# First and last batch of a two-layer graph kernel in another order: weights by block, first x split on other engines, last attention re-ordered

## The reference

```
# layer 0:  Wi, Wj = W[:, :D], W[:, D:]        a = adj as float, deg = a.sum(1)
x = ln(x + deg * (x @ Wi.T + b) + a @ (x @ Wj.T))
# layer 1: 8 heads of 64, mask where adj == 0, scores / 8
q, k, v = x @ Wq.T + bq, x @ Wk.T + bk, x @ Wv.T + bv
p = softmax(where(adj == 0, -inf, q k.T / 8))
x = ln(x + (p v) @ Wo.T + bo)
```

## Time and profile before

| | us |
|---|---|
| median of 3 runs (3036.11 to 3036.71) | 3036.34 |
| the profiled execution's own time | 3034.67 |
| its span, first to last instruction | 3032.9 |
| PE busy in the span | 2974.3 (98%) |
| DVE / ACT / POOL busy | 2316.6 / 1729.0 / 1636.7 |
| mean granted TensorE clock | 0.992 |

### The profile page before, as it was taken

The page is one execution under the profiler, slowest core; times in us unless marked ns, Lnnn a source line. Parts: engine busy times, 40 slices in busy tenths (PEclk is TensorE's granted clock), DMA queues, the critical chain, the costliest instruction groups (busy, mean ns, idle before and its releaser), DMA issues.

```text
span 3032.9 us, 61054 instructions
## 1 busy us (share of the span) xinstructions
PE 2974.3 (98%) x20096; PEld 2618.4 (86%) x20096; DVE 2316.6 (76%) x5909; ACT 1729.0 (57%) x4620; POOL 1636.7 (54%) x1545
## 2 busy tenths in 40 slices
PE   5999999999999999999999999999999999999996
PEld 4888888888888888888888888888888888888886
DVE  6777777777777777777777777777777777777775
ACT  3555565565565555555655655555555556556554
POOL 5455555455555565555554555555655555545542
PEclk8999999999999999999999999999999999999998
DMA  3010100101101101101001011001001010010100
GB/s 125 29 42 28 35 35 28 41 28 35 41 28 35 41 28 35 41 28 35 32 30 41 28 35 41 28 35 41 28 35 36 33 35 29 33 41 28 35 29 22
DMA packets 48428, 108.37 MB, mean 36 GB/s; under 512 B 3600, under 2 KB 4112, under 8 KB 48400
## 3 DMA queue, kind: packets, MB, share of 16 engines
q1 hardware_dynamic: 48400, 108.02, 10.3%
HBM read 74.46 MB, written 33.55 MB: 36 GB/s over the span
## 4 chain that ended last, share of the span: by engine, by line
PE 97%; DVE 1%; issue 0%; ACT 0%; DMA 0%; POOL 0%; SPq 0%; POOLq 0%; DVEq 0%
PE proj L417 52%; PE proj L459 21%; PE av L417 8%; PE attn L575 7%; PE attn L563 7%; PE proj L513 2%; DMA w_raw<-in_w0T 0%; DVE wji_lo L1077 0%; ACT probs L719 0%; DVE probs L896 0%; DVE t_raw L1066 0%; DVE mj_mi L971 0%; DVE pT_lo L918 0%; DVE mj_mi L977 0%; DVE wq_lo L1082 0%
## 5 line engine op out<-in xcount | busy, mean ns | idle before, releaser
L719 ACT ACTIVATE probs<-probs,exp_bias 128x256 f32<-128x256 f32 x1024 | 508.0, 498 | 41.7 <-DVE exp_bias L904 40.6
L735 ACT CAST pT_hi<-attn 128x512 fp32r<-128x512 f32 x512 | 275.0, 588 | 379.8 <-PE av L417 318.7
L317 POOL TENSOR_TENSOR probs<-probs,row_inv 128x512 f32<-128x512 f32 x256 | 264.4, 1043 | 395.7 <-DVE row_inv L914 395.7
L918 DVE TENSOR_TENSOR pT_lo<-attn,pT_hi 128x512 fp32r<-128x512 f32 x512 | 328.7, 683 | 87.2 <-ACT pT_hi L735 85.2
L459 PE MATMUL proj<-wji_hi,xs_hi 128*128 128x512 f32 x896 | 363.4, 406 | 20.5 <-DVE wji_lo L1077 17.3
L896 DVE CUSTOM_DVE_ANT_0 probs<-attn,mask_add 128x256 f32<-128x256 f32 x1024 | 376.4, 419 | 6.3 <-PE attn L563 3.8
L459 PE MATMUL proj<-wji_lo,xs_hi 128*128 128x512 f32 x896 | 355.8, 397 | 0.0
L459 PE MATMUL proj<-wji_hi,xs_lo 128*128 128x512 f32 x896 | 355.7, 397 | 0.0
L928 DVE SCALAR_TENSOR_TENSOR oT<-av,bv_cols,o_part 64x256 f32<-64x256 f32 x512 | 243.4, 475 | 120.7 <-POOL oT_lo L345 60.5
L743 ACT COPY o_part<-av 64x512 f32<-64x512 f32 x256 | 149.5, 584 | 319.8 <-PE av L417 318.3
L345 POOL TENSOR_TENSOR oT_lo<-oT,oT_hi 128x256 fp32r<-128x256 f32 x256 | 201.6, 787 | 209.1 <-ACT oT_hi L750 209.1
(11 more groups left out here) (110 smaller groups left out, 8629.5 us busy)
## 6 DMA issues: line engine op xcount, KB each, us to landing
xs_raw<-in_xT SPq DMA_DIRECT2D x64, 512.0 KB, 3.3
xb<-in_x SPq DMA_DIRECT2D x64, 512.0 KB, 3.3
out<-hb SPq DMA_DIRECT2D x64, 512.0 KB, 2.8
w_raw<-in_w0T SPq DMA_DIRECT2D x2, 1024.0 KB, 7.2
stage<-in_wqT SPq DMA_DIRECT2D x1, 1024.0 KB, 12.3
stage<-in_wkT SPq DMA_DIRECT2D x1, 1024.0 KB, 14.5
stage<-in_wvT SPq DMA_DIRECT2D x1, 1024.0 KB, 5.3
stage<-in_woT SPq DMA_DIRECT2D x1, 1024.0 KB, 5.4
```

The lines of the kernel that those rows point to most:

```text
L317: pool.tensor_tensor(probs[:, g % 2, 1, :, :], probs[:, g % 2, 1, :, :], row_inv[:, g % 2, R:2 * R].unsqueeze(2).to_broadcast([P, R, N]), ...
L719: last = nc.scalar.activation(e, e, ACT.Exp, bias=exp_bias[:, g % 2, s:s + 1], scale=SCALE, accum_out=row_sum[:, g % 2, s:s + 1])
L735: nc.scalar.copy(pT_hi[:, i, :, :], attn[2 * (g % 2) + i][:, :].rearrange("p (k q) -> p k q", k=R)).then_inc(pt_hi_done, 1)
L918: V.tensor_tensor(pT_lo[:, i, :, :], attn[2 * (g % 2) + i][:, :].rearrange("p (k q) -> p k q", k=R), pT_hi[:, i, :, :].bitcast(F32), ALU.s ...
```

## The change

Head: `w0T` is loaded in four blocks of two DMAs of 256 KB each, each block with a semaphore of its own, and ACT and DVE wait for the block that they use. ACT makes the high halves of the first x, DVE its sums and low halves; POOL has no part in it. DVE splits weight block 0 before the first weight sum, and makes `deg` and `deg_b0` after the fourth `first_sum` instead of before the first. ACT makes wq's high half before `first_copy(0, 1)`. Of wq's low half POOL does one half of the columns after both `mi_add`, and DVE the other after the norm. The low halves of wv and wo stand one place later in DVE's list.

Tail: pairs 1 and 3 of the last batch write their transposed probabilities to a second pair of buffers (`mj_hi`, `mj_lo`, free by then), so `pt_high` need not wait for the `attend` before it. The second pair of heads' maxima stand before the first inverse sums; both y products come before the first transposes; the scores of pairs 2 and 3 are issued apart; on POOL `normalise_odd(b, 2)` stands before `split_o(b, 1)`.

```diff
+    W_LOADS = ((0, 0), (0, 1), (1, 1), (1, 0))
...
+        pT_tail = [(pT_hi, pT_lo), tuple(t[:, :, :].rearrange("p r (a n) -> p r a n", a=2) for t in (mj_hi, mj_lo))]
...
             load_xT(0)
-            for kind in range(2):
-                sp.dma_start(w_raw[:, kind, :, :], w0T[(1 - kind) * D:(2 - kind) * D, :].rearrange(
-                    "(c p) o -> p c o", p=P)).then_inc(w_loaded["wji"], 16)
+            for i, (kh, oh) in enumerate(W_LOADS):
+                for kind in range(2):
+                    at = (1 - kind) * D + kh * HD
+                    sp.dma_start(w_raw[:, kind, 2 * kh:2 * kh + 2, oh * HD:(oh + 1) * HD],
+                                 w0T[at:at + HD, oh * HD:(oh + 1) * HD].rearrange("(c p) o -> p c o", p=P)).then_inc(
+                                     block_loaded[i], 16)
...
-            sum_x(0)
-            for part in range(2):
-                x_high(0, part)
-                x_low(0, part)
+            mj_low_row1(0)
             pool.wait_ge(deg_b0_ready, R)
             add_bias(0)
-            mj_low_row1(0)
+            pool.wait_ge(mi_added, R)
+            pool.wait_ge(w_hi_done, 1)
+            pool.tensor_tensor(w_lo[WEIGHTS[0]][:, 0:2, :], stage[0][:, 0:2, :],
+                               w_hi[WEIGHTS[0]][:, 0:2, :].bitcast(F32), ALU.subtract).then_inc(w_half_split, 1)
             root("h", 0)
...
                 if not (first and pair == 0):
-                    pe.wait_ge(pt_read, 2 * (G * b + 2 * pair))
-                for g in (2 * pair, 2 * pair + 1):
+                    pe.wait_ge(pt_read, 2 * (G * b + pairs[-1] - 1))
+                for g in pairs:
...
             def last_step(b):
                 scores(b, 0)
                 y(b - 1, 0, tail=True)
+                y(b - 1, 1, tail=True)
                 transpose_p(b, 0, 0)
                 transpose_p(b, 0, 1)
-                attend(b, 0)
                 transpose_p(b, 1, 0)
                 transpose_p(b, 1, 1)
-                y(b - 1, 1, tail=True)
-                scores(b, 1)
-                attend(b, 1)
+                scores(b, 1, only=2)
+                attend(b, 0)
+                scores(b, 1, only=3)
+                attend(b, 1, tail=True)
...
-                    act.wait_ge(av_done, G * b + g)
+                    act.wait_ge(av_done, G * b + g - (1 if tail else 0))
...
-                    act.wait_ge(w_loaded["wji"], 32)
+                    act.wait_ge(block_loaded[(0, 3, 2)[blk]], 32)
...
+            for part, blocks in enumerate((slice(1, 4), slice(4, 8))):
+                if part == 0:
+                    act.wait_ge(xT_loaded, 16)
+                else:
+                    act.wait_ge(xs_summed, 4)
+                nc.scalar.copy(xs_hi[:, blocks.start - 1:blocks.stop - 1, :, :],
+                               xs_raw[:, blocks, :, :]).then_inc(xs_hi_done, 1)
             for i in range(4):
                 high_block(i)
...
+            split_weight(0)
             first_copy(0, 1)
-            split_weight(0)
...
+            dve.wait_ge(xT_loaded, 16)
+            x_ = lambda i: xs_raw[:, i, :, :]
+            V.tensor_tensor(x_(4), x_(0), x_(3), ALU.add).then_inc(xs_summed, 1)
+            V.tensor_tensor(x_(6), x_(1), x_(0), ALU.subtract).then_inc(xs_summed, 1)
...
+            x_low(0)
+            x_low(1)
+            low_block(0)
             sum_blocks(0)
-            low_block(0)
             sum_blocks(1)
...
             norm_apply("h", 0, h_row)
-            split_weight(1)
+
+            dve.wait_ge(w_hi_done, 1)
+            dve.wait_ge(w_half_split, 1)
+            V.tensor_tensor(w_lo[WEIGHTS[0]][:, 2:4, :], stage[0][:, 2:4, :], w_hi[WEIGHTS[0]][:, 2:4, :].bitcast(F32),
+                            ALU.subtract).then_inc(w_split, 1)
             hT_low(0, 0)
             hT_low(0, 1)
-            split_weight(2)
+            split_weight(1)
```

More of the change, by code:

```diff
@@ L549, in v, with scores @@
                 rows_times_w("v", r, hT_hi, hT_lo, "wv")
-            def scores(b, pair, first=False):
+            def scores(b, pair, first=False, only=None):
                 pe.wait_ge(read["q"], 2 * b + pair + 1)
                 pe.wait_ge(read["k"], 2 * b + pair + 1)
+                pairs = (2 * pair, 2 * pair + 1) if only is None else (only,)
                 if not (first and pair == 0):
-                    pe.wait_ge(pt_read, 2 * (G * b + 2 * pair))
-                for g in (2 * pair, 2 * pair + 1):
+                    pe.wait_ge(pt_read, 2 * (G * b + pairs[-1] - 1))
+                for g in pairs:
                     terms = [(q_hi, k_hi), (q_lo, k_hi), (q_hi, k_lo)]
@@ L577, in transpose_p, with attend @@
                 last.then_inc(pt_done, 1)
-            def attend(b, g, first=False):
+            def attend(b, g, first=False, tail=False):
                 if g == 0:
@@ L586, in attend @@
                 for i in range(2):
-                    terms = [(kt, half) for kt in range(R) for half in (pT_hi, pT_lo)]
+                    terms = [(kt, half) for kt in range(R) for half in pT_tail[g % 2 if tail else 0]]
                     for j, (kt, half) in enumerate(terms):
@@ L729, in normalise_even, with pt_high @@
                 last.then_inc(norm_even_done, 1)
-            def pt_high(b, g, i, first=False):
+            def pt_high(b, g, i, first=False, tail=False):
                 act.wait_ge(pt_done, 2 * (G * b + g) + i + 1)
                 if i == 0 and not (first and g == 0):
-                    act.wait_ge(av_done, G * b + g)
-                nc.scalar.copy(pT_hi[:, i, :, :],
+                    act.wait_ge(av_done, G * b + g - (1 if tail else 0))
+                nc.scalar.copy(pT_tail[g % 2 if tail else 0][0][:, i, :, :],
                                attn[2 * (g % 2) + i][:, :].rearrange("p (k q) -> p k q",
@@ L830, in last_step @@
                 normalise_even(b, 1)
+                pt_high(b, 1, 0, tail=True)
+                pt_high(b, 1, 1, tail=True)
                 o_low_part(b, 0)
-                pt_high(b, 1, 0)
-                pt_high(b, 1, 1)
+                exponentials(b, 2)
                 o_high(b, 0)
-                exponentials(b, 2)
+                normalise_even(b, 2)
                 o_low_part(b, 1)
-                normalise_even(b, 2)
                 exponentials(b, 3)
+                pt_high(b, 2, 0, tail=True)
+                pt_high(b, 2, 1, tail=True)
                 o_high(b, 1)
-                pt_high(b, 2, 0)
-                pt_high(b, 2, 1)
                 normalise_even(b, 3)
                 o_low_part(b, 2)
-                pt_high(b, 3, 0)
-                pt_high(b, 3, 1)
+                pt_high(b, 3, 0, tail=True)
+                pt_high(b, 3, 1, tail=True)
                 o_high(b, 2)
@@ L914, in inverse_sums, with pt_low @@
                 V.reciprocal(row_inv[:, g % 2, :], row_sum[:, g % 2, :]).then_inc(inv_done, 1)
-            def pt_low(b, g, i):
+            def pt_low(b, g, i, tail=False):
+                high, low_ = pT_tail[g % 2 if tail else 0]
                 dve.wait_ge(pt_hi_done, 2 * (G * b + g) + i + 1)
-                V.tensor_tensor(pT_lo[:, i, :, :],
+                V.tensor_tensor(low_[:, i, :, :],
                                 attn[2 * (g % 2) + i][:, :].rearrange("p (k q) -> p k q", k=R),
-                                pT_hi[:, i, :, :].bitcast(F32), ALU.subtract).then_inc(pt_read, 1)
+                                high[:, i, :, :].bitcast(F32), ALU.subtract).then_inc(pt_read, 1)
             def o_sum(b, g, first=False):
@@ L1069, in sum_blocks @@
                 else:
+                    dve.wait_ge(block_loaded[3], 32)
                     dve.wait_ge(t_done, 2)
@@ L1135, in last_step @@
                 maxima(b, 0)
+                maxima(b, 1)
                 inverse_sums(b, 0)
-                maxima(b, 1)
                 y_sum(b - 1, 0, 0)
+                norm_stats("out", b - 1, 0, read["y"], hb_row[0])
                 inverse_sums(b, 1)
+                y_sum(b - 1, 1, 0)
                 pt_low(b, 0, 0)
                 pt_low(b, 0, 1)
-                norm_stats("out", b - 1, 0, read["y"], hb_row[0])
+                norm_stats("out", b - 1, 1, read["y"], hb_row[0])
+                maxima(b, 2)
+                pt_low(b, 1, 0, tail=True)
+                pt_low(b, 1, 1, tail=True)
                 o_sum(b, 0)
-                pt_low(b, 1, 0)
-                pt_low(b, 1, 1)
-                maxima(b, 2)
                 inverse_sums(b, 2)
@@ L1149, in last_step @@
                 o_sum(b, 1)
+                pt_low(b, 2, 0, tail=True)
+                pt_low(b, 2, 1, tail=True)
                 inverse_sums(b, 3)
-                pt_low(b, 2, 0)
-                pt_low(b, 2, 1)
-                y_sum(b - 1, 1, 0)
-                norm_stats("out", b - 1, 1, read["y"], hb_row[0])
+                norm_mean("out", b - 1)
                 o_sum(b, 2)
-                norm_mean("out", b - 1)
-                pt_low(b, 3, 0)
```

(3 more changed lines are left out.)

47 lines of the change are left out of this document (31 added, 16 removed).

## The result

The changed kernel takes **3074.78 us** (median of 4 runs, 3073.29 to 3075.30), the kernel before 3036.53 beside it: ratio 1.0125, 95% interval 1.0108 to 1.0143. The forecast was 3019.3 with a range of 3014.5 to 3025.5. It is wrong in its sign, and 55.5 us off.

A forecast was written before the change was run, and what follows sets the result against it. The prediction took PE to bound the kernel nearly end to end, with waits only in head and tail. Gains of 9.85 us (head) and 7.2 (tail), 17.05 together, gave 3019.3 us, range 3014.5 to 3025.5.

The forecast's parts named there:

- First product: Head: with weights in four blocks, the first matmul moves from 14.60 to 9.55, a gain of 5.05 us.
- Products: Head, the seven products: last done at 25.75, 16.2 us after the first matmul instead of 21.8; gain 5.6 us.
- Products to norm: Head, last product to layer norm: 11.9 us instead of 11.0 because of the moved work, -0.9 us; norm at 37.6.
- the prediction's middle: Head: end of `mi_add` taken at 32.4, between 32.0 without and 32.9 with POOL delaying `deg_b`.
- its case with the delay: Head: POOL's `mj_low_row1` starts ahead of `deg_b` and delays it by 1.26 us, `mi_add` ends at 32.9; a coin toss.
- Norm to q: Head, layer norm to first q: 3.4 us instead of 3.5, a gain of 0.1 us.
- q to scores: Head, first q at 41 to first `scores` at 59.5, with no wait on wo.
- Tail: Last step: gain 7.2 us (bounds 5.5 to 10), mainly from earlier scores of pair 2 and no 3.5 us POOL wait.
- (a): Rival, low clock: PE at 1.2 GHz pace through products 3 to 6 and in the tail; gain 11.9, 3024.5 us; chance 0.13.
- (b): Rival: the tail gives nothing because ACT's chain of exponentials, casts and copies sets it; gain 9.85, 3026.5 us; chance 0.08.
- (c): Rival, head: wo's low half on DVE and POOL's `add_bias(1)` block each other; 3023.3 us; chance 0.06.
- (d): Rival, slower: engines enter the loop with another spacing, every step pays; at 0.4 us a step 3043.7 us; chance 0.03.

The follow-up runs named there:

- the three kernels with 24 memsets and the column last: Head's part, whole change, whole with earlier degree reduction; each with 24 dummy memsets ahead of DVE's stream, their column behind all tensors: 3026.21, 3018.99, 3017.64 us.
- a_end24: Changed kernel plus 24 unused one-element memsets ahead of DVE's first instruction, their column behind all tensors: 3018.99 us, ratio 0.9945 to the kernel before.
- head_pad24: Changed kernel with the tail of the kernel before, plus 24 memsets ahead of DVE's first instruction, column behind all tensors: 3026.21 us, ratio 0.9969.
- The runs with 11 and with 24 memsets: Unused memsets ahead of DVE's first instruction: 11 in the kernel before, 3076.04 us; 24 in the changed kernel, 3020.10 us (column in front) or 3018.99 (column last).
- with 4 memsets: Kernel before plus 4 unused memsets ahead of DVE's first instruction, addresses unchanged (DVE's loop at 170 to 449): 3126.29 us, single run.
- with 26: Kernel before plus 26 unused memsets ahead of DVE's first instruction, addresses unchanged (DVE's loop at 192 to 471): 3207.38 us, single run.
- 27: Kernel before plus 27 unused memsets ahead of DVE's first instruction, addresses unchanged (DVE's loop at 193 to 472): 3035.92 us, single run.

## Why the prediction was wrong

**The step that failed** is the condition under its first paragraph: a microsecond won at the ends is won in full "if the loop keeps its pace". It did not. I took the loop as untouched because none of its instructions changes, and PE waits for nobody in it. What changed was where DVE's loop lies in DVE's stream: 11 instructions further back, past an edge of a block, at 55.8 us. Every term of the sum was about work and waits between engines; none was about the code itself.

In the prediction's first paragraph the 17.3 us in two waits for low halves already hold the 14.60 until the first matmul; they don't come on top of it. No term of the sum used it.

**First product**, 5.05 forecast, 4.65 measured: block 0 was seen at 7.6 instead of 5.8, so ACT's high half of it ended at 8.6 instead of 8.15, and the low half followed closely. In the three kernels with 24 memsets and the column last ACT started on block 0 at 6.7 to 6.9, and the first matmul came at 9.2 to 9.3. **Products**, the last done near 26.1 against 25.75: right. **Products to norm**: the norm came at 37.98 instead of 37.6, with `deg_b` delayed by POOL; `mi_add` ended at 32.6, between the prediction's middle (32.4) and its case with the delay (32.9). **Norm to q**: 3.46 us against 3.4. **q to scores** took 19.4 against the 18.5 forecast; this and the 0.4 of the first product are what the head lacks in that trace. PE waits for nobody in these 19.4 us. Its 120 matmuls ran longer at the lower clock: 3.1 us behind the first q the clock is 0.50 in the changed kernel, and 0.98 in the kernel before.

```profile
44.50:46.50 2.00, 2.00 (x12) 2.00 (x11) 0.00 (x0) 1.76 (x1) 1.92 (x2) 0.50 0.45 112
```

```profile
54.00:56.00 2.00, 2.00 (x19) 2.00 (x19) 0.57 (x1) 0.46 (x2) 1.92 (x2) 0.98 0.88 336
```

It comes and goes from one execution to the next: a_end24, with the same head, needed 18.6, head_pad24 again 19.5. The same head alone with the loop well placed measured 10.1.

**Tail**: right to 0.1, 0.3 and 0.2 us at its three marks (12.8, 24.1 and 45.6 against 12.7, 23.8 and 45.4), and the lower clock came where forecast:

```profile
3053.00:3059.00 6.00, 4.60 (x22) 4.20 (x22) 3.46 (x6) 2.06 (x4) 1.70 (x4) 0.50 0.00 0
```

Of that row's figures the 0.50 matters: PE's granted clock is the 1.2 GHz level behind a pause of 3.41 us, as in the earlier trace rows.

**Sum**: 17.05 forecast, 17.2 measured with 24 memsets (3018.99 against the forecast time of 3019.3). That the two agree to 0.2 is in part luck: by the traces the head of a_end24 gained 9.05 (60.44 against 69.49) and its tail 6.8 (45.8 against 52.6), 15.9 together, and the measured difference has an interval of 12.8 to 20.9. The working held within it; what it left out did not.

**Rivals.** (a) and (b) did not happen in the changed kernel; in a_end24 the low clock did last until 21.2, into the products that (a) names, and its head gained 9.05 all the same. (c) did not happen either: DVE's `wo_lo` took 3.75 us beside POOL's `add_bias`, but PE waited for nobody before the first `scores`. (d) had the right side and the right place, a wait in every turn of the loop, but the wrong mechanism: spacing. The runs with 11 and with 24 memsets refute it, since they change no order. Its price (0.4 us a step) was also too small: 0.96. The sentence that a PE wait inside the loop would make the prediction wrong at its root was the right thing to watch, and a chance of 0.03 for all that could slow the loop was too low: I had asked only which instruction could be late, not whether the loop's instructions are there at all.

## What to carry to other kernels

When a change adds or removes instructions ahead of a hardware loop, count each engine's stream: the length of the loop and its place modulo 256, with what stands ahead of the program (63 for DVE here). In this case a body of 280 was whole only in some places, and a few cheap instructions ahead of it moved it there. A profile in which the packets on an instruction queue grow with the turns of the loop tells of it at once (13 against 157). And before two versions are compared by a few tenths of a per cent, check that their tensors lie at the same addresses, or try two or three shifts of both.

## What the runs showed of the hardware

- A branch back over the edge of a block cost DVE 2.77 us in the changed kernel, 3.71 with 4 memsets, and 3.03 and 2.25 in a row with 26, and the whole kernel 1.6 to 5.9 us a turn (mean steps of 46.97 and 49.14, less 46.18, twice).
- PE's granted clock stayed at 1.00 behind a pause of 1.54 us in the loop and was 0.50 behind one of 3.66 us.
- The edges are sharp to one instruction and lie 256 instructions apart: slow from 4 memsets, whole again from 27. The two lines of 256 instructions in the Trainium skill's page "Runtime: NRT & Kernel Launch", section "Instruction fetch mechanics", fit both edges; no run here tests the other engines.
- PE's loop of 685 instructions stood at the same place in the two kernels, and no wait of PE at its branch shows in the lists.
- Moving half of SBUF's tensors by 32 to 128 bytes changed the time by -15.4 to +10.3 us, at a mean granted clock of 0.991 to 0.992 in the profiled executions.
